# Cross-attention and FFN: the order of each engine's work in the front, written out tile by tile

## The reference, cut to what matters

```
def _L0_xattn_ref(x_query, x_key, x_value, Wq, bq, Wk, bk, Wv, bv, Wo, bo):
    q, k, v = proj(Wq, bq, x_query), proj(Wk, bk, x_key), proj(Wv, bv, x_value)   # einsum('oi,bil->bol') + b
    # 8 heads of 64 columns
    p = softmax(einsum('hbdk,hbek->hbde', qh, kh) / 8)
    x = einsum('hbde,hbek->hbdk', p, vh)          # heads put together again
    return proj(Wo, bo, x)

def _L0_ffn_ref(x, gate_w, gate_z, gate_s, ...):
    w = (w_int - zeros) * scales                  # gate, up: 512 x 1792; down: 1792 x 512
    return (silu(x @ gate) * (x @ up)) @ down

x = x + xattn(layernorm(x), ctx, ctx, ...)
x = x + ffn(layernorm(x), ...)
```

## Time and profile before

| what | value |
|---|---|
| runs | 438.23, 441.49, 441.42 us; median 441.42 |
| profiled execution, its span | 438.38 us, 436.6 us |
| busy: TensorE, VectorE, ScalarE, GpSimd | 413.0 (95%), 330.2 (76%), 330.9 (76%), 265.7 us (61%) |
| first matmul of the main loop | 49.24 us after the start of the span |
| DMA | 35.44 MB, mean 81 GB/s |

### The profile page before, as it was taken

The page is one execution under the profiler, slowest core; times in us unless marked ns, Lnnn a source line. Parts: engine busy times, 40 slices in busy tenths (PEclk is TensorE's granted clock), DMA queues, the critical chain, the costliest instruction groups (busy, mean ns, idle before and its releaser), DMA issues.

```text
span 436.6 us, 10758 instructions
## 1 busy us (share of the span) xinstructions
PE 413.0 (95%) x4234; PEld 318.7 (73%) x4234; DVE 330.2 (76%) x582; ACT 330.9 (76%) x540; POOL 265.7 (61%) x264
## 2 busy tenths in 40 slices
PE   7878988999997999999999999999999999999994
PEld 4655666776865778677777787687887888888872
DVE  3877657999779876877887776877887666677676
ACT  2246898887976878687778878687978998988970
POOL 2256677899597655755565756744576555555561
PEclk9989999999999999999999999999999999999999
DMA  7466984865852000000110001000010000001003
GB/s 229 128 192 178 336 305 152 288 233 179 234 178 72 2 2 26 2 26 18 59 50 26 0 2 26 8 20 26 2 50 1 2 1 0 26 24 50 1 1 96
DMA packets 26793, 35.44 MB, mean 81 GB/s; under 512 B 1871, under 2 KB 18423, under 8 KB 26743
## 3 DMA queue, kind: packets, MB, share of 16 engines
q1 hardware_dynamic: 26354, 34.69, 24.8%
q10 hardware_dynamic: 324, 0.07, 0.1%
q0 software_dynamic: 64, 0.00, 0.0%
HBM read 30.56 MB, written 4.19 MB: 80 GB/s over the span
## 4 chain that ended last, share of the span: by engine, by line
PE 67%; DMA 10%; issue 6%; POOL 6%; DVE 5%; SPq 2%; ACT 2%; POOLq 0%; DVEq 0%; ACTq 0%
PE banks L760 20%; PE banks L762 18%; PE banks L773 10%; PE banks L774 9%; DMA z_in<-in_L_ffn_up_z 4%; PE banks L658 2%; DMA wgu_in<-in_L_ffn_gate_w 2%; DVE yT L1006 2%; DMA z_in<-in_L_ffn_gate_z 2%; DMA wgu_in<-in_L_ffn_up_w 2%; POOL t_sb L417 1%; PE banks L698 1%; PE banks L676 1%; PE banks L687 1%; POOL wgu_in L410 1%
## 5 line engine op out<-in xcount | busy, mean ns | idle before, releaser
L556 ACT ACTIVATE banks<-banks,ratio 128x512 f32<-128x512 f32 x336 | 208.0, 663 | 35.5 <-PE banks L762 26.0
L1006 DVE SCALAR_TENSOR_TENSOR yT<-banks,sd,yT 128x512 f32<-128x512 f32 x208 | 154.2, 747 | 48.7 <-PE banks L774 48.1
L760 PE MATMUL banks<-xT,wgu 128*128 128x512 f32 x448 | 182.1, 406 | 4.6 <-DVE t_sb L991 3.7
L762 PE MATMUL banks<-xT,wgu 128*128 128x512 f32 x448 | 175.1, 391 | 0.0
L417 POOL TENSOR_TENSOR t_sb<-t_sb,u_sb 128x512 f32<-128x512 f32 x56 | 72.4, 1292 | 63.0 <-DVE t_sb L991 62.8
L760 PEld LDWEIGHTS banks<-xT,wgu 128*128 128x128 f32 x448 | 84.1, 188 | 26.4 <-issue 3.7
L762 PEld LDWEIGHTS banks<-xT,wgu 128*128 128x128 f32 x448 | 84.3, 188 | 15.3
L773 PE MATMUL banks<-hr,wd 128*128 128x512 f32 x224 | 89.3, 399 | 4.6 <-DVE yT L1006 2.7
L774 PE MATMUL banks<-hr,wd 128*128 128x512 f32 x224 | 87.5, 390 | 0.0
L430 POOL TENSOR_TENSOR hr<-t_sb,hr 128x512 fp32r<-128x512 f32 x56 | 73.2, 1307 | 5.1 <-ACT hr L578 0.7
L773 PEld LDWEIGHTS banks<-hr,wd 128*128 128x128 f32 x224 | 42.0, 188 | 19.7 <-DVE yT L1006 9.9
(11 more groups left out here) (93 smaller groups left out, 387.5 us busy)
## 6 DMA issues: line engine op xcount, KB each, us to landing
x_sb<-in_x SPq DMA_DIRECT2D x16, 256.0 KB, 5.5
out<-x_sb SPq DMA_DIRECT2D x16, 256.0 KB, 2.0
wgu_in<-in_L_ffn_gate_w SPq DMA_DIRECT2D x7, 512.0 KB, 6.3
z_in<-in_L_ffn_gate_z SPq DMA_DIRECT2D x7, 512.0 KB, 4.5
wgu_in<-in_L_ffn_up_w SPq DMA_DIRECT2D x7, 512.0 KB, 6.3
z_in<-in_L_ffn_up_z SPq DMA_DIRECT2D x7, 512.0 KB, 4.6
wd_in<-in_L_ffn_down_w SPq DMA_DIRECT2D x7, 512.0 KB, 5.7
z_in<-in_L_ffn_down_z SPq DMA_DIRECT2D x7, 512.0 KB, 5.2
```

The lines of the kernel that those rows point to most:

```text
L556: act.activation(banks[:, bank, :], banks[:, bank, :], ACT.Copy, scale=ratio[:, m, g, it:it + 1]).then_inc(done[n % 2], 1)
L760: pe.matmul(banks[:, bank, :], w, xT[:, c % 2, 0, g, :], start=g == 0, stop=False, skip_group_check=True)
L762: pe.matmul(banks[:, bank, :], w, xT[:, c % 2, 1, g, :], start=False, stop=True, skip_group_check=True).then_inc(full[n % 2], 1)
L1006: dve.scalar_tensor_tensor(y, bank, sd[:, it, b:b + 1], y, ALU.mult, ALU.add).then_inc(s_free, 1)
```

## The change

The four loops of the front are replaced by lists written out, with other orders: the statistics of tiles 0 to 3 stand ahead of the first `most`, those of tile 4 near the end; `residual`, `values` and `score` of neighbouring tiles are placed anew; `take_qk(4, 1)` stands behind the last rows of tile 3. `copy_predicated` moves from `prepare` into `divide`, and `divide` from the second tile to the end of the front. The filler goes from 50 matmuls to 37. The transposes of the scales stand before the first `score`, and have a semaphore of their own. `project(4)` writes banks 2 and 3, and the wait for `take_qk(4)` moves to step n = 1. On the SP queue Wk is first, x and ctx of tiles 0 to 3 stand ahead of the weights, and for five pieces weights, zero points and one tile of x or ctx are issued together and then waited for. The removed lines of the four loops are left out below; they are in the listing above.

```diff
+    PACED = 5
...
-        s_tr, s_wT, s_prep, s_scl, s_low, s_brow, s_bqk = (
+        s_tr, s_tr2, s_trs, s_wT, s_prep, s_scl, s_low, s_brow, s_bqk = (
...
             if kind == "QK":
-                return 0 if t <= PRE else 6
+                return 0 if t < PRE else 2 if t == PRE else 6
...
+            sync.dma_start(wraw[:, 1, :], Wk).then_inc(s_wsm, 16)
             for t in range(2):
                 load_x(t)
                 load_ctx(t)
             load_x(2)
+            load_x(3)
             sync.dma_start(s_raw[0:NG * NI, 0, :], gate_s.rearrange("g (t p) -> (g t) p", p=P)).then_inc(s_sc, 16)
             sync.dma_start(s_raw[NG * NI:2 * NG * NI, 0, :],
                            up_s.rearrange("g (t p) -> (g t) p", p=P)).then_inc(s_sc, 16)
             sync.dma_start(s_raw[0:NI * NC, 1, :], down_s.rearrange("g (t p) -> (g t) p", p=P)).then_inc(s_sc, 16)
             load_ctx(2)
-            load_x(3)
-
-            for k in range(EARLY):
+            load_ctx(3)
+
+            for k in range(PACED):
                 load_w(k)
-                if 1 <= k < 3:
-                    (load_ctx if k == 1 else load_x)(k + 2)
+                load_zeros(k)
+                if k >= 1:
+                    (load_x if k % 2 else load_ctx)(PRE + (k - 1) // 2)
                 sync.wait_ge(s_w[k], 16)
-                load_zeros(k)
-                if k == 2:
-                    load_ctx(PRE)
                 wait_zeros(sync, k)
-            load_x(PRE + 1)
-            load_ctx(PRE + 1)
-            for k in range(EARLY, NP):
+            for k in range(PACED, NP):
                 load_w(k)
                 if k in CTX_AT:
                     load_ctx(CTX_AT[k])
                 load_zeros(k)
-                if 4 <= k < 4 + NT - PRE - 2:
-                    load_x(PRE - 2 + k)
+                if k < PACED + NT - PRE - 2:
+                    load_x(PRE + 2 + k - PACED)
...
+            for t in range(PRE):
+                rstd(0, t)
+            weigh(0)
+            less_zeros(0)
+            raised()
+            weigh(1)
+            rstd(1, 0)
+            less_zeros(1)
+            weigh(2)
+            rstd(1, 1)
+            weigh(3)
+            less_zeros(2)
+            rstd(1, 2)
+            rstd(0, 4)
+            rstd(1, 3)
+            ratios()
+            less_zeros(3)
...
-            load(s_wsm, wraw[:, 1, :], Wk)
...
-                    act.wait_ge(s_tr, t + 2)
+                    act.wait_ge(s_tr2, 1)
+                    act.wait_ge(s_trs, 1)
...
+            act.wait_ge(s_trs, 1)
+            ng = 2 * NG * NI
+            act.copy(flat(sg), banks[:, 4, 0:ng]).then_inc(s_scl, 1)
+            act.copy(sd[:, :, :].rearrange("p g c -> p (g c)"), banks[:, 4, ng:ng + NI * NC]).then_inc(s_scl, 1)
+            norm1(2)
+            power_of(0)
+
+            act.wait_ge(s_wT, 3)
+            take_v(0)
+            norm1(3)
+            take_a(0)
+            power_of(1)
+            take_v(1)
+            convert(0)
+            take_a(1)
+            power_of(2)
+            take_v(2)
+            norm2(0)
+            power_of(3)
+            take_a(2)
+            take_x(0)
+            norm2(1)
+            convert(1)
+            take_v(3)
+            take_x(1)
+            take_a(3)
+            convert(2)
+            norm2(2)
+            norm1(4)
+            take_x(2)
...
-                    if n == 0:
+                    if n == 1:
+
                         pe.wait_ge(s_qk, 2 * (PRE + 1))
-                    if n == 1:
-                        pe.wait_ge(s_sub, PRE)
...
-            stir(8)
+            stir(6)
...
-            stir(5)
+            pe.wait_ge(s_sc, 48)
+            ng, nd = 2 * NG * NI, NI * NC
+            pe.transpose(banks[:, 4, 0:ng], s_raw[0:ng, 0, :], ident[0:ng, 0:ng])
+            pe.transpose(banks[:, 4, ng:ng + nd], s_raw[0:nd, 1, :], ident[0:nd, 0:nd]).then_inc(s_trs, 1)
+            stir(1)
...
-            mm.then_inc(s_tr, 1)
+            mm.then_inc(s_tr2, 1)
+            stir(2)
+            pe.wait_ge(s_qk, 4)
+            project(2)
+            pe.wait_ge(s_wT, 3)
+            values(0)
+            stir(1)
+            pe.wait_ge(s_sub, 1)
+            score(1)
+            pe.wait_ge(s_v, 1)
+            mix(0)
+            stir(2)
+            apply(0)
+            stir(2)
+            pe.wait_ge(s_x1, 1)
+            values(1)
+            stir(1)
+            pe.wait_ge(s_qk, 6)
+            project(3)
+            pe.wait_ge(s_sub, 2)
+            score(2)
+            stir(2)
+            pe.wait_ge(s_v, 2)
+            mix(1)
+            stir(2)
+            apply(1)
+            stir(1)
+            pe.wait_ge(s_sub, 3)
+            score(3)
+            pe.wait_ge(s_x1, 2)
+            values(2)
+            stir(3)
+            pe.wait_ge(s_v, 3)
+            mix(2)
+            pe.wait_ge(s_scl, 2)
+            turn_x(0)
+            stir(1)
+            apply(2)
+            stir(2)
+            pe.wait_ge(s_x1, 3)
+            values(3)
+            turn_x(1)
+            stir(1)
+            pe.wait_ge(s_v, 4)
+            mix(3)
+            stir(2)
+            apply(3)
+            stir(3)
+            turn_x(2)
+            pe.wait_ge(s_sub, PRE)
+            project(PRE)
+            stir(1)
...
-            stir(3, U_BANK[1])
+            stir(3, U_BANK[0])
...
+                if t == PRE - 1:
+                    dve.wait_ge(s_p, t)
...
+            def divide():
                 dve.wait_ge(s_pr, 4)
                 dve.wait_ge(s_low, 1)
                 dve.copy_predicated(flat(sp_), flat(big), flat(sg)).then_inc(s_pr, 1)
 
-            def divide():
                 dve.wait_ge(s_pr, 5)
...
+            stats(0, 0)
             take_w(0)
+            shift(0, 0)
             dve.wait_ge(s_brow, 1)
             dve.tensor_copy(bqk[:, :, :].rearrange("p m o -> p (m o)"), banks[:, 7, 0:2 * D]).then_inc(s_bqk, 1)
+            stats(0, 1)
+            stats(0, 2)
             dve.wait_ge(s_bqk, 1)
             take_qk(0, 0)
             take_qk(0, 1)
+            shift(0, 1)
+            stats(0, 3)
+
+            most(0)
+            shift(0, 2)
+            less_max(0)
+            take_qk(1, 0)
+            take_w(1)
+            dve.tensor_copy(bvo[:, :], banks[:, 7, 4 * D:4 * D + 2]).then_inc(s_wT, 1)
+            invert(0)
+            take_qk(1, 1)
+            shift(0, 3)
+            prepare()
+            most(1)
+            dve.wait_ge(s_wT, 3)
+            residual(0)
+            less_max(1)
+            take_qk(2, 0)
+            take_qk(2, 1)
+            invert(1)
+            stats(1, 0)
+            most(2)
+            take_qk(3, 0)
+            less_max(2)
+            take_qk(3, 1)
+            residual(1)
+            invert(2)
+            most(3)
+            shift(1, 0)
+            less_max(3)
+            stats(1, 1)
+            invert(3)
+            shift(1, 1)
+            residual(2)
+            rest_x(0)
+            stats(1, 2)
+            stats(0, 4)
+            rest_x(1)
+            shift(1, 2)
+            residual(3)
+            shift(0, 4)
+            stats(1, 3)
+            divide()
+            shift(1, 3)
+            rest_x(2)
+            take_qk(4, 0)
...
+            take_qk(4, 1)
```

More of the change, by code:

```diff
@@ L820, in _ @@
                                    start=True, stop=True)
-            mm.then_inc(s_tr, 1)
-            pe.wait_ge(s_sc, 48)
-            ng, nd = 2 * NG * NI, NI * NC
-            pe.transpose(banks[:, 4, 0:ng], s_raw[0:ng, 0, :], ident[0:ng, 0:ng])
-            pe.transpose(banks[:, 4, ng:ng + nd], s_raw[0:nd, 1, :], ident[0:nd, 0:nd]).then_inc(s_tr, 1)
-            for j in range(PRE):
-                if j + 1 < PRE:
-                    stir(1)
-                    pe.wait_ge(s_sub, j + 1)
-                    score(j + 1)
-                if j + 2 <= PRE:
-                    pe.wait_ge(s_qk, 2 * (j + 2))
-                    project(j + 2)
-                if j == 0:
-                    pe.wait_ge(s_wT, 3)
-                else:
-                    stir(1 if j < PRE - 1 else 2)
-                    pe.wait_ge(s_x1, j)
-                values(j)
-                if j >= 2:
-                    if j == 2:
-                        pe.wait_ge(s_scl, 2)
-                    turn_x(j - 2)
-                stir(2)
-                pe.wait_ge(s_v, j + 1)
-                mix(j)
-                stir(2)
-                apply(j)
@@ L1018, in _ @@
             dve.memset(warm[:, 0:1], 0.0).then_inc(s_warm, 1)
-            stats(0, 0)
-            shift(0, 0)
             def take_w(i):
-                dve.wait_ge(s_tr, i + 1)
+                dve.wait_ge((s_tr, s_tr2)[i], 1)
                 m = slice(2 * i, 2 * i + 2)
@@ L1034, in _ @@
             take_qk(0, 1)
-            stats(0, 2)
-            for j in range(PRE):
-                most(j)
-                if j + 2 <= PRE:
-                    shift(0, j + 2)
-                less_max(j)
-                if j + 1 < PRE:
```

(31 more changed lines are left out.)

46 lines of the change are left out of this document (1 added, 45 removed).

## The result

The changed kernel took 435.60 us (median of 7 runs, 434.04 to 437.22); the kernel before, with the runs made beside it, 439.16 us (7 runs, 438.23 to 441.49). The ratio is 0.9896 with a 95% interval of 0.9869 to 0.9922: about 1% faster. The profiled executions took 434.57 and 438.38 us, with spans of 432.8 and 436.6 us.

What follows compares the result with a forecast made beforehand. VectorE was taken to bound the front, TensorE the loop. Gains 1.9 + 4.2 - 0.5 = 5.6 us, less 0.8, plus 0.4, gave 5.2 off 438.38: 433.2; between that and 436.3 at the upper level, 434.7 us, range 431 to 439.5.

Steps and rivals of the forecast that it cites:

- Part 1, up to the first `most`: Start of the front: earlier `project(0)` and less filler ahead of `score(0)` gain 1.9 us, bounds 0 and 2.6.
- Part 2, from `most(0)` to the loop: Rest of the front: VectorE work moved out and less idle time gain 4.2 us, bounds 1.7 and 6.
- The added waits: Front's paced loads: pieces land at about 14, 20, 26, 32 and 38 us, with a margin of 7 us.
- The move of `take_qk(4, 1)`: End of the front: putting it behind the last tile takes VectorE work out of the stretch, a gain of 0.7 us.
- Part 3, the seam: Where front meets loop: later `divide` makes `convert(3)` end 2.0 us after the loop's first matmul, loss 0.8 us.
- Part 4, piece 6: Early loop: zero points landing near 46 us remove waiting there, gain 0.4 us, between 0 and 1.2.
- Part 5, the clock: TensorE in the front: less filler may worsen the clock; 0.5 us lost, between 1.2 gained and 2 lost.
- A: The forecast itself, whole kernel: gains of 3.8 to 7.5 us, 431 to 437.6 us; chance 0.52.
- B: Front: late data or a half-clock stretch leaves a gain of 2 to 3.5 us, 435 to 439; chance 0.28.
- C: Loop takes the front's gain back, limited by the weights' stream: gain 0 to 2 us, 437 to 441; chance 0.12.
- D: Slower: TensorE stays at 1.2 GHz through the front, 443.4 us if up to its end; chance 0.08.

Runs made afterwards that it cites:

- serial_pace: The changed kernel with the zero points of the five paced pieces issued only after their weights landed, as before the change; 441.66 us, ratio 1.0004.
- old_queue: The changed kernel with the SP queue of the kernel before, all engine lists as changed; 439.12 us, ratio 0.9973.
- qk_early: The changed kernel with `take_qk(4, 1)` put back ahead of the last two subtractions of tile 3; 435.28 us, ratio 0.9856.
- both_hold3: The changed kernel with `divide` and `ratios` moved earlier, `raised` ahead of `less_zeros(0)`, and piece 3 issued only after `score(2)`; 433.87 us, ratio 0.9829.
- divide_early: The changed kernel with `divide` moved up behind `most(1)` and `ratios` behind `less_zeros(1)`; 433.47 us, ratio 0.9822.
- both_moves: The changed kernel with `divide` and `ratios` moved earlier and `raised` ahead of `less_zeros(0)`; 436.37 us, ratio 0.9866.
- after_again: The changed kernel timed once more without any edit; 436.19 us, ratio 0.9897 to the kernel before.
- new_queue: The kernel before with only the new order of the SP queue, all engine lists as before; 437.92 us, ratio 0.9935.
- no_filler: The changed kernel without the 26 fillers between the first score and the last tile's transposes; 436.13 us, ratio 0.9869.
- hold3: The changed kernel with one wait added on SP, so that piece 3 is issued only after `score(2)`; 435.18 us, ratio 0.9852.
- raised_first: The changed kernel with GpSimd's `raised` moved ahead of `less_zeros(0)`; 435.28 us, ratio 0.9846.
- fill_gap: The changed kernel with six fillers instead of two ahead of `project(2)`; 436.23 us, ratio 0.9867.

## Why the prediction was right or wrong, point by point

The forecast was 434.7 us in a range of 431 to 439.5; measured 435.60. For an execution like the profiled one it was a gain of 5.2 us, and 3.8 was measured; between the medians it is 3.6. The mechanism was right, two terms of the sum were too small. That the time was off by 0.9 us and the gain by 1.6 is some luck: the forecast took the kernel before at 439.9 us, between its two levels, and its median came out at 439.16.

- **Part 1, up to the first `most`: right.** `project(0)` forecast at 7.2, measured 7.23; `most(0)` at 12.0, measured 11.89. The statistics of tiles 1 and 2 did not hold up `take_qk(0)`.
- **Part 2, from `most(0)` to the loop: the mechanism right, the size wrong.** The steps that I named are there: no wait for tile 4, `rstd` down to 0.6 us, waits of 1.04 us for `score(1)` (0.9 forecast) and of 1.43 for `apply(0)` (1.4). The first of these agrees by luck: `score(1)` was late by the slow clock, and VectorE was late too, by the `tensor_scalar` that GpSimd held up for 1.84 us; in serial_pace, with the same held instruction but at full clock, VectorE does not wait for `score(1)` at all. The stretch took 33.6 us, and 31.6 was forecast. From `most(0)` to `residual(0)` it took 10.43 us, against 9.05 in serial_pace and 9.18 in old_queue, which ran at full clock from 14 and 16 us on: 1.3 us for the clock, where the sum had 0.5. From `residual(0)` to `most(2)` it took 5.66 us, against 4.29 and 4.30: 1.4 us for a term that the sum didn't have, TensorE's gap by issue, 1.07 us at `score(2)`, behind which `most(2)` waited 1.33 us. The 0.8 us too little for the clock and the 1.4 for the gap are the 2 us that the stretch was longer. serial_pace starts its loop at 43.33, 5.9 us ahead of the kernel before, where 5.6 was forecast. The trace of before had a gap of this kind, 0.8 us in `apply(0)`, and I had read over it:

```profile
22.14 0.58 PE L698 MATMUL banks<-v_sb,aT 64*64 64x64 f32 x25 [0.80 <-issue]
```

- **The added waits: right.** The pieces behind the first were issued at 13.8, 19.4, 25.3, 32.0 and 37.1 us, when the one before had landed; 14, 20, 26, 32 and 38 was forecast. GpSimd waited for none of them in the front.
- **The move of `take_qk(4, 1)`, 0.7 us: too large.** Taken back it cost 0.2 us in qk_early, because 0.44 us of idle time stands in the same place. I counted the work and the idle time behind it both as gains.
- **Part 3, the seam: right.** `convert(3)` was to end 2.0 us after the loop's first matmul and ended 2.2 after it; the loss of 0.8 was 0.64 us at the second `gate_up` and 0.9 at `gated`. both_hold3 shows that it is real and can be had back: its second `gate_up` has no wait, and step 0 keeps the whole lead of the front. In divide_early and both_moves the wait went too, and a gap by issue of 0.9 and 1.2 us in the burst took its place.
- **Part 4, piece 6: the landing right, the effect elsewhere.** Its zero points were issued at 39.24 us, and none took longer than 8.0 us to land, so they were there by 47.3. VectorE no longer waits for them, but TensorE's stall of 1.17 us at step 2 stands as before, 1.16 us at 56.74, released by ScalarE's conversion. The steps 6 to 10 then gained 0.9 us. Part of it is a wait of 0.47 us of TensorE for GpSimd at 93.71 us of the kernel before, which the changed kernel does not have. The same gain is in after_again (from 0.1 us behind the kernel before to 1.0 ahead), in new_queue (0.8) and in serial_pace (1.0), and less of it in divide_early (0.4) and both_moves (0.1). Since serial_pace has the pairs undone, it does not come from them; what else it comes from is open.
- **Part 5, the clock: 0.5 us taken, 1.3 lost in the front, within the bounds of 1.2 gained and 2 lost.** By the rows the full clock came at about 13 us, as in the kernel before, and the half clock came back for 3 to 4 us. after_again and both_moves had the case of the bound of 2 us, full clock first from 19.5 us on.
- **Rivals.** A held, at its lower edge (3.8 to 7.5 us). B lies beside it: its mechanism, a stretch at half clock between 17 and 25 us, happened as well, and 435.60 us is within both ranges, so the time does not tell the two apart. C did not come, but had a real mechanism behind it: with the old pacing (serial_pace) the loop takes back all that the front saves. The earlier stream of data, which I had set against it, is what kept it away. D did not come, and its condition, half clock through the whole front, did not arise in any profile.

## What to carry to other kernels

A front that ends earlier is worth only what the data of the loop behind it allow: check when the first pieces after the front are wanted, not only those that it uses itself. Lay the new lists side by side with the durations of the trace; that was good to 0.3 us where nothing else interfered. Add a term for TensorE's gaps by issue in a stretch of many small matmuls, read the start of the kernel for slow rows and not only the clock column, and don't count both a piece of work and the idle time next to it.

## What the runs showed of the hardware

**GpSimd holds back a small VectorE instruction.** The `tensor_scalar` of 28 elements took 0.18 us with GpSimd idle, 1.84 us when GpSimd's subtraction of 2.37 us had started 0.6 us before it, and it ended 0.05 us after that subtraction. It was 1.84 or 1.85 us in every profile with `less_zeros(0)` ahead of `raised`, and 0.18 us in the three without. In the kernel before it took 0.60 us and ended, at 18.92, 0.03 us after GpSimd's `weigh(0)`. So the row of before already showed a held instruction, not its own length. The Trainium skill (GPSIMD Engine Reference, Specifications) says that GpSimd shares its SBUF interfaces with VectorE and that instructions of some modes contend; the traces agree, and give the price: up to the rest of the GpSimd instruction that is running. GpSimd's row in the changed kernel, then the two rows of the kernel before:

```profile
16.43 2.37 POOL L409 TENSOR_TENSOR wgu_in<-wgu_in,z_in 128x1024 int32<-128x1024 int32 x1
```

```profile
17.85 1.04 POOL L392 TENSOR_TENSOR e_sb<-e_sb,ri 128x512 f32<-128x512 f32 x1 [4.41 <-DVE ri L941]
18.32 0.60 DVE L976 TENSOR_SCALAR fl<-fl 128x28 f32<-128x28 f32 x1
```

**TensorE has gaps by issue in front of the same small matmuls again and again.** In the front, the nine profiles of written-out lists with paired loads and filler had 0.2 to 2.2 us of them, nearly all at the last matmuls of `score(2)` and at those of `apply(0)`, and new_queue, with the old lists, 3.3 us. Where weights and zero points came one after the other there were 0.8 (the kernel before), 0.2 (serial_pace) and none (old_queue). no_filler, with paired loads, had none either, with fewer instructions in the list. The gap at one place in one kernel was 1.07 us in one execution and 1.91 in another. So they were longer where more was being loaded, but a part of them has another cause: hold3 and both_hold3 had 0.53 and 0.25 us at `score(2)` with a DMA share of 0.01 and 0.00 in the same 2 us. What TensorE waits for there is not shown.

**TensorE's clock rose and fell in different places in executions of one kernel, and the clock column misses the start.** It fell at 16 to 20 us in one profile of the changed kernel and at 29 to 34 in the other. The column reads 1.00 until its first fall, but 32 matmuls of 64 x 64 took 1.13 or 1.14 us at 7 to 9 us in the changed kernel and in all its variants but raised_first, as long as at a granted clock of 0.50 (1.13 at 11.38 us in raised_first), and 0.69 us later on, where the column is 1.00 again. By these rows the clock first rose at about 13 to 14 us in the changed kernel's first profile, serial_pace, divide_early, hold3, both_hold3 and qk_early, and at about 19 us in after_again, fill_gap, no_filler and both_moves.
